# Last batch of an adaLN block: where the exponential, the x1 normalisation, the rests of the probabilities and one feed-forward output stand in their queues

## The reference

```python
x = hidden_states                       # 4 batches x 1024 tokens x 512
mod = (silu(c) @ wmod).reshape(4, 6, 1, 512)
sa, ca, ga, sb, cb, gb = ...            # ga, gb bounded away from 0
h = layernorm(x) * (1 + ca) + sa
x = x + ga * attention(h)               # one score matrix, 1024 x 1024, shared by 16 heads
h = layernorm(x) * (1 + cb) + sb
x = x + gb * ((einsum('btd,rde->bte', h, factors)) / sqrt(8) + bias)
```

## Time and profile before

| | us |
|---|---|
| median of 3 runs | 464.22 |
| lowest, highest | 464.06, 466.62 |
| profiled execution | 464.78 |
| its span, first to last instruction | 463.0 |
| busy: PE, PEld | 450.1 (97%), 365.1 (79%) |
| busy: DVE, ACT, POOL | 365.9 (79%), 338.8 (73%), 237.7 (51%) |

### The profile page before, as it was taken

How to read it: one execution, slowest core, us unless ns; L and a number is a source line. 1 busy time by engine, 2 the same in 40 slices (tenths; PEclk the granted TensorE clock), 3 DMA queues, 4 the chain that set the end, 5 groups by cost and what they waited for, 6 DMA issues and landing times. The chain is left out here.

```text
span 463.0 us, 7344 instructions
## 1 busy us (share of the span) xinstructions
PE 450.1 (97%) x2114; PEld 365.1 (79%) x2114; DVE 365.9 (79%) x641; ACT 338.8 (73%) x676; POOL 237.7 (51%) x307
## 2 busy tenths in 40 slices
PE   8989999999999999999999999999999999999996
PEld 5768778788888888888888888888888777777674
DVE  5988879678777878789787987798887577887765
ACT  5889777687868777778787786878786566567552
POOL 0347546152555554455565645454644475566662
PEclk9999999999999999999999999999999999999999
DMA  7999999634678365867677366877674237565512
GB/s 288 382 356 218 158 177 170 141 74 132 183 206 271 92 206 159 264 203 241 195 195 228 110 216 190 258 201 245 185 227 115 91 117 227 158 217 180 183 58 91
DMA packets 79160, 88.07 MB, mean 190 GB/s; under 512 B 4872, under 2 KB 55816, under 8 KB 79120
## 3 DMA queue, kind: packets, MB, share of 16 engines
q1 hardware_dynamic: 75168, 80.00, 56.5%
q0 software_dynamic: 3808, 7.34, 9.6%
q10 hardware_dynamic: 144, 0.26, 0.2%
HBM read 53.49 MB, written 34.10 MB: 189 GB/s over the span
## 5 line engine op out<-in xcount | busy, mean ns | idle before, releaser
L1470 POOL TENSOR_SCALAR ve<-mv 128x1 f32<-128x1 f32 x64 | 22.5, 351 | 165.7 <-DVE mv L1173 120.1
L464 PE MATMUL ps_o<-v_lo,pt_hi 128*128 128x512 f32 x256 | 100.2, 391 | 0.9 <-DVE pt_lo L1062 0.9
L466 PE MATMUL ps_o<-v_hi,pt_hi 128*128 128x512 f32 x256 | 99.7, 389 | 0.0
L465 PE MATMUL ps_o<-v_hi,pt_lo 128*128 128x512 f32 x256 | 99.6, 389 | 0.0
L1062 DVE TENSOR_TENSOR h_lo<-h_f,h_hi 128x512 fp32r<-128x512 f32 (+1 forms) x67 | 49.7, 741 | 12.2 <-ACT h_hi L728 11.6
L464 PEld LDWEIGHTS ps_o<-v_lo,pt_hi 128*128 128x128 f32 x256 | 48.0, 188 | 12.9 <-issue 2.9
L466 PEld LDWEIGHTS ps_o<-v_hi,pt_hi 128*128 128x128 f32 x256 | 48.0, 188 | 10.1
L465 PEld LDWEIGHTS ps_o<-v_hi,pt_lo 128*128 128x128 f32 x256 | 48.1, 188 | 9.7
L756 ACT ACTIVATE h_f<-x1b,mod_t 128x128 f32<-128x128 f32 x120 | 53.1, 596 | 2.8 <-DVE x1b L1191 2.5
L464 PE MATMUL ps_y<-f_lo,h_hi 128*128 128x512 f32 (+1 forms) x124 | 48.7, 393 | 2.3 <-issue 1.5
L465 PE MATMUL ps_y<-f_hi,h_lo 128*128 128x512 f32 (+1 forms) x124 | 47.9, 386 | 0.0
(11 more groups left out here) (201 smaller groups left out, 1032.2 us busy)
## 6 DMA issues: line engine op xcount, KB each, us to landing
x_blocks<-xn SPq DMA_DIRECT2D x50, 256.0 KB, 2.7
p_blocks<-probs SPq DMA_DIRECT2D x24, 512.0 KB, 3.6
pb<-p_blocks SPq DMA_DIRECT2D x96, 128.0 KB, 3.2
x_ring<-in_x SPq DMA_DIRECT2D x16, 512.0 KB, 4.6
x1b<-x_blocks SPq DMA_DIRECT2D x30, 256.0 KB, 2.9
result<-x_ring SPq DMA_DIRECT2D x15, 512.0 KB, 3.0
f_sum<-in_factors POOLq DMA_DIRECT2D x14, 512.0 KB, 6.2
xb<-x_blocks SPq DMA_DIRECT2D x20, 256.0 KB, 2.9
```

What stands on the lines that cost most here:

```text
L464: nc.tensor.matmul(acc, a_hi, b_lo, start=first, stop=False)
L465: nc.tensor.matmul(acc, a_lo, b_hi, start=False, stop=False)
L466: return nc.tensor.matmul(acc, a_hi, b_hi, start=False, stop=last)
L1470: nc.gpsimd.tensor_scalar(ve[:, one], mv[:, u, 1:2], EPS, None, ALU.add).then_inc(ve_done, 1)
```

## The change

On ACT, in step 23, `ffn_out(20)` is put ahead of `pair_q(13)`. In the closing steps the order after `ffn_out` becomes `modulate_x1(t - 2)`, `exponentials(t + 2)`, `h2_upper(t - 2)`, `normalize_x1(t - 1)`; step 31, which has `normalize_last_x1`, keeps that one first.

On DVE, the rests of the probabilities are put ahead of `add_x` and `x1_stats`, and `pair_q(13)` moves from the end of step 23 to behind `row_max(25)` in step 24.

On SP, the closing steps get an order of their own: `send_p(t + 2)` is put ahead of `send_x1(t - 1)`, the store and `fetch_x1(t - 1)`, where it was behind them. No instruction is added or removed, and PE's and POOL's queues stay as they are.

```diff
--- before.py
+++ after.py
@@ -436,7 +436,22 @@
                     sp.wait_ge(y_stored, 16 * (g - 1))
                     load_x(g - 2 + 2 * PB)
 
-            for t in range(T):
+            def closing_step(t):
+                g, u = t // 2, t % 2
+                if scored_last_in(t - 1) is not None:
+                    send_p(scored_last_in(t - 1))
+                if t + 1 < T:
+                    fetch_p(t + 1)
+                if scored_in(t) is not None:
+                    send_p(scored_in(t))
+                if t < T - 1:
+                    send_x1(t - 1, 1 - u)
+                if u:
+                    store_pair(g - 2)
+                if t < T - 1:
+                    fetch_x1(t - 1, 1 - u)
+
+            for t in range(T - TB):
                 if t == 1:
                     sp.wait_ge(mod_acc, GB + 1)
                     load_x(6)
@@ -446,6 +461,8 @@
                     store_gate(1, GB)
                 if t == 3:
                     spread_gate(1, 0)
+            for t in range(T - TB, T):
+                closing_step(t)
             last = PAIRS - 1
             store_pair(last - 1)
             for half in range(2):
@@ -901,9 +918,11 @@
                         normalize_x(q + 1, u)
                     else:
                         normalize_x_blocks(q + 1, u)
+                if t == T - TB - 1:
+                    ffn_out(t - 3)
                 if queries_in(t) is not None:
                     pair_q(queries_in(t))
-                if t >= 3:
+                if 3 <= t < T - TB - 1:
                     ffn_out(t - 3)
 
             def closing_step(t):
@@ -916,12 +935,12 @@
                 ffn_out(t - 3)
                 if t == T - 1:
                     normalize_last_x1(t - 1, 1 - u)
-                else:
-                    normalize_x1(t - 1, 1 - u, False)
                 modulate_x1(t - 2, batch_of((t - 2) // 2))
-                h2_upper(t - 2)
                 if scored_in(t) is not None:
                     exponentials(scored_in(t))
+                h2_upper(t - 2)
+                if t < T - 1:
+                    normalize_x1(t - 1, 1 - u, False)
 
             def vector_upper(v, k):
 
@@ -1236,17 +1255,18 @@
                 if ahead_of_gate is not None:
                     ahead_of_gate()
                 gate_attention(t, u, batch_of(g))
-                if queries_in(t) is not None:
+                if queries_in(t) is not None and t < T - TB - 1:
                     pair_q(queries_in(t))
 
             def closing_step(t):
                 u = t % 2
                 if scored_last_in(t - 1) is not None:
                     row_max(scored_last_in(t - 1))
+                    pair_q(queries_in(t - 1))
+                probs_rest(t, 0)
+                probs_rest(t, 1)
                 add_x(t - 1)
                 x1_stats(t - 1, 1 - u)
-                probs_rest(t, 0)
-                probs_rest(t, 1)
                 turn_x1(t - 2)
                 invert_sum(t, u)
                 if queries_in(t) is not None:
```

## The result

The changed kernel takes 473.37 us (median of 4 runs, 471.54 to 475.48) beside 464.42 us for the kernel before (4 runs); the ratio is 1.0172, with a 95% interval of 1.0133 to 1.0211. The forecast was 468.0 us in a range of 464.0 to 472.0: the direction and the mechanism are as predicted, the size is more than twice the forecast, and the time lies outside the range. The profiled executions are 464.78 before and 472.78 after, their spans 463.0 and 471.0; the 8.0 us between them are what the traces have to explain. The ratio makes 8.0 us too; the medians are 9.0 us apart.

A forecast was written before the change was run, and what follows sets the result against it. PE was taken to bound the kernel up to the last batch, then a 10.70 us ring: six rounds and the last passage move tile 31's gate from 449.15 to 452.9, adding 3.75 us; forecast 468.0 us, range 464.0 to 472.0.

The forecast's parts named there:

- the ring: Closing steps: normalise x1, send, fetch, turn, modulate, exponential, h2_upper, next normalise; each round lasts at least 10.70 us.
- the send to fetch of 2.80: SP, issue of the x1 send to issue of its fetch: 2.80 us, bounds 2.46 and 3.72.
- the ACT part of a round: Round without transfers: normalisation to send 0.91, turn and ACT start 0.73, modulate 1.80, exponential 1.11, h2_upper 0.53 us.
- the cover of `turn_p`: DVE: turn_p ends 9.7 us after normalisation began, ahead of the high part of h2 at 10.8, so it costs nothing.
- the pause of 0.83 us: PE in step 24, feed-forward product waiting for ffn_out(20); ffn_out ahead of pair_q(13) was to remove its 0.83 us.
- the 10.4 to 11 us that I named as the sign: Trace after: normalisations of x1 that far apart from step 25 on; 9.1 to 9.5 apart would show the forecast wrong.
- rival (c): x1 send behind the 512 KB send takes 3.72 us, 0.92 more in seven passages: 474.4 us, halfway 471.2; chance 0.18.
- My estimate of 5.2 us for two transfers: x1 send plus fetch, 256 KB at 2.6 us each, instead of 5.62: round 10.28 us, result 3 us lower.
- issue of the fetch to the turn: Fetch of x1b on SP until DVE's turn: 2.82 us per passage, upper bound a tenth above the slowest for crowding.
- last passage from turn to gate: Step 31: turn begins 449.07, modulate 449.80, h2_upper 451.60, then h2_rest(29) 0.66 us; DVE gates tile 31 at 452.9.
- Part (3): DVE: attend's rests 1.77 us earlier, moments 1.18 us later, covered by 3.4 us of ACT work ahead of normalisation.
- rival (d): Only step 24 counts, ACT's order without effect: gain at most 1.3 us, 462.9 us; chance 0.15 shared with the no-change rival.

The follow-up runs named there:

- the run with the cut transfers: Whole change, but closing steps fetch x1b from long-stored x blocks before both sends, so nothing reads the sent x1: 464.93 us, ratio 0.9997 to the kernel before.
- the other kernels with the ring: Kernel before with only the ACT reorder and its SP order, 475.99 us; changed kernel with longer modulation, 480.04; with 48 or 120 extra PE waits, 474.58 and 478.84.
- 48 waits: Changed kernel plus 48 waits on a long-reached semaphore in PE's prologue, to move PE's code loads earlier: 474.58 us, ratio 1.0212 to the kernel before.

## Why the prediction was wrong in size

**What held.** The bound and the ring, the place where it starts (379.70 for 379.45), the exponential of tile 25 (371.06 for 370.6, where the scores came 0.9 us later than before), the send to fetch of 2.80 (2.76 on average), the ACT part of a round (six rounds less their transfers last 29.3 us, forecast 29.4), the cover of `turn_p` but in step 30, where it came 0.3 us late, and the pause of 0.83 us that went. Two of these agree by luck. The start of the ring is 0.25 us off only because the 0.9 us by which this execution was late beforehand met a passage that was 0.6 us quicker than my sum. And in the 29.3 us the exponential followed the modulation after 1.57 us in three of five rounds, where I had 1.80, but after 2.14 in the first, where it waited for DVE's maximum behind the copy of the queries, a way that my sum did not have. Of the six intervals, three lay in the 10.4 to 11 us that I named as the sign (10.39, 10.81, 10.48); the others were 12.20, 12.11 and 9.83. The sends did not collide as in rival (c). The rule of the Trainium skill, page "DMA: Bandwidth & Descriptors", section "Rules for kernel authors", to issue early and wait late, fits the run with the cut transfers: 8 us between waiting for a transfer at once and having issued it 6.2 to 7.4 us ahead of its use, though there with data that need not be waited for. My estimate of 5.2 us for two transfers, from the figures of its section "Anatomy of one DMA" for GpSimd's path, is 0.9 less than the 6.1 us that the seven passages on SyncE took on average; the measurement decides.

**What failed** is the step "issue of the fetch to the turn ... I take 2.82; bounds 2.5 and 3.1". The seven sum to 23.17 us, forecast 19.74: 3.43 us. Of these, 3.19 are the three fetches into which a code load fell. The sum had no term for them, although the page of the kernel before lists the 17 packets of queue 8. Tile 31's gate came 3.99 us later than forecast, and the terms are: start of the ring +0.25, sends -0.27, fetches +3.43, last passage from turn to gate 4.47 for 3.83 or +0.64, mostly the rest of h2, 1.19 for 0.66 with POOL's additions beside it; together 4.05. The bounds of 2.5 and 3.1 came from the seven fetches of the closing steps. Over all thirty fetches of x1b in that trace the spread is wider:

```profile
DMA to landing us min/median/max: 2.5/2.9/3.8
```

Five of them took 3.2 to 3.8 us, so the wider range was on view. Their mean is 2.92, though, and would have added 0.8 of the missing 3.4 us: in none of the thirty had a load started 0.6 to 1.5 us behind the issue. In the change all three loads did, in the other kernels with the ring one or two of three. That it was all three is chance as far as the record shows.

The 8.0 us of the traces and the 9.0 of the medians differ because the profiled execution after lay 0.6 us under its kernel's median, and the one before 0.4 over its own. The other three executions after had a mean granted clock of 0.992 to 0.993, this one 0.996, so they spent more time at the lower level; what that cost them is not shown.

**Part (3)**, rests ahead of `add_x`, I called covered. In the whole change it is, since DVE waits for x1b anyway; alone, that edit costs 1.06%. And the sentence that before the change a normalisation "waited for nothing that came from the previous one's transfers" is wrong: it waits for the gate, and the gate stands on DVE behind `turn_p` and the fetch of the probabilities. Today's steps of 9.4 us are a ring already, which rival (d) and the sum left out.

## What to carry to other kernels

Before moving an instruction on an in-order engine, follow its result to the same instruction of the next step. If the way leads back, the sum of that way is the least length of a step, whatever the busy shares say, and a transfer pair through DRAM was the longest piece of it here. Every microsecond in such a ring counts once a round, so the mean of its transfers with their slow ones has to be taken, from the whole trace and with what else will be under way: here fetches with an instruction load behind their issue, or a store just ahead, took 3.3 to 4.6 us instead of 2.9. Orders that look wasteful, a normalisation ahead of a modulation that could already run, may be what keeps a ring open.

## What the runs showed of the chip that was not expected

The slow fetches beside code loads are one. The other is the clock. In the fourth round PE had paused 2.9 us by its weight loads; the next eight matmuls followed each other at 0.43 us and then at 0.23 again:

```profile
424.93 0.69 PE L557 MATMUL ps_s<-k_both,qs_lo 128*128 128x512 f32 x1 [2.51 <-ACT probs L821]
425.42 0.63 PE L558 MATMUL ps_s<-k_both,qs_hi 128*128 128x512 f32 x1
...
428.65 0.39 PE L483 MATMUL ps_y<-f_hi,h_hi 128*128 128x512 f32 x1
428.88 0.39 PE L481 MATMUL ps_y<-f_lo,h_hi 128*128 128x512 f32 x1
```

The granted clock, the column ahead of the DMA share, was 0.50 there, the lower level of 1.2 GHz, and 1.00, the upper one of 2.4 GHz, behind it:

```profile
425.00:428.40 3.40, 3.40 (x8) 2.64 (x9) 3.06 (x5) 2.05 (x4) 0.00 (x0) 0.50 0.74 231
428.40:432.00 3.60, 3.60 (x17) 2.98 (x16) 1.26 (x4) 0.60 (x1) 1.81 (x4) 1.00 0.52 150
```

The pauses of 1.97 and 2.02 us at 382 and 446 us did not bring it down in this execution. The length of a pause alone does not tell whether it will: with 48 waits the clock stayed up behind one of 2.46 us at 414.6 and fell behind one of 2.37 at 426.3. The eight slow matmuls cost PE 8 x 0.20 = 1.6 us. Little of it can have reached the end: in the next step PE's weight loads paused 1.15 us ahead of the feed-forward product, and no wait in the ring's next round was for PE.
